# A relative-position attention, two causal stages and two mixtures: the second attention's scores in 64-row strips of high and low parts

## The chip, the cores and the metric

The kernel runs on one core of one Trainium2 chip. The metric is device time in microseconds (us); lower is better. Engines: TensorE (matmul, PE in the rows; PEld is its weight load), VectorE (DVE), ScalarE (ACT), GpSimd (POOL) and SyncE (SP, which issues most DMAs). They run on their own instruction streams and meet on semaphores.

## The reference

Input x is 4 batches of 512 tokens of 256 values. Four stages follow one another: an attention with relative positions against a context, a layer of causal attention and a mixture of 8 experts (2 per token), a cross attention with 16 heads of 64, and a mixture of 16 experts (6 per token). The change is in the causal attention of the second stage:

```python
def _causal_attention(nx, Wqkv, bqkv, Wo, bo):
    qkv = nx @ Wqkv + bqkv
    q, k, v = jnp.split(qkv, 3, axis=-1)           # each 16 heads of 16
    scores = jnp.einsum('bqhd,bkhd->bhqk', q, k) / jnp.sqrt(jnp.float32(HEAD_DIM))
    scores = jnp.where(causal, scores, jnp.finfo(scores.dtype).min)
    attn = jax.nn.softmax(scores, axis=-1)
    out = jnp.einsum('bhqk,bkhd->bqhd', attn, v).reshape(B, S, D)
    return out @ Wo + bo
```

nx is the layer norm of the first attention's result (with its residual). Inputs and outputs are float32.

## The kernel before

The second attention works in 16 units (NJ): four heads of one batch each, numbered n = 4 x batch + group. A unit has eight steps (NUF). Two sets of score products exist for each unit:

- the *natural rows*: queries on partitions, keys along the columns. Only their row maxima are used. VectorE takes them with one custom instruction per head and row block (`row_max`, L2101) into a tile MX. They run 12 steps (AHEAD) before the other set.
- the *transposed scores* (key products): keys on partitions, queries along the columns. ScalarE takes exp of them from PSUM into PTf (`exp_f`, L1686), and `values_f` (L1046) multiplies PTf with the values; a column of ones gives the sums.

The maxima reach the transposed scores through the contraction. A head has 16 values but sits in a strip of 32 rows: rows 16 to 31 hold the other head of the pair as zeros, a constant -1 in KP, and the maxima in QP. `max_to_rows` (L1071) turns MX on TensorE, and VectorE adds it into QP (L2106).

In `scores_f` (L1026, L1031) a step issues four fp32 matmuls, two heads of the transposed scores and two of the natural rows, each in a strip of 32 rows, so that the four run side by side. F_ROWS orders the natural row blocks so that a step's natural rows are as wide as its transposed scores:

```python
F_ROWS = (1, 1, 0, 0, 3, 3, 2, 2)
keys_mm = mm(STB[(2 * s + x) % 3][:, 0:S - c * P], KP[o:o + HQ8, hg, ...], QP[n % 4][o:o + HQ8, c * P:S], ...)
rows_mm = mm(PD[g % 2][:, x, 0:w], QP[m % 4][o:o + HQ8, r * P:r * P + P], KP[o:o + HQ8, hg, b * S:b * S + w], ...)
```

Banks: two pairs (PD[0], PD[1]) hold natural rows, three (STB) transposed scores, and one (MB) everything else in the order of the list M_USES: projections, values, turned maxima (`mx`), turned outputs (`ot`). TensorE waits before a step's key products for the first exponential of the step before (`f_ex`), and before natural rows for the maxima that free their banks (`f_max`). Every engine's order is written out by hand; at steps P_STEP, OT_STEP, MX_STEP and those of H_STEP1, H_STEP7 and Q_STEP the loop issues values, turned outputs, turned maxima and projections of later units: queries (`queries_f`, for two units at a time), keys (`hk`), values (`hv`), normalised tokens (`h`). A projection for keys or queries (L806) is copied from the bank by ScalarE twice, with one of two head masks (L1608, L1615).

GpSimd applies the causal mask to the diagonal of PTf (L718, `f_ca`), and in units 2 to 9 it also computes the residual Hs of the second stage behind every second mask (L707, L710). Before the stage it adds the first attention's outputs to X (L695). SP loads the projection weights WFs, WFv while the first attention ends, and all expert weights once the last scores are done (`f_st`). The first keys and queries (`f_hw`, `f_hr`) are projected within the last steps of the first attention (n == NJ in its loop), each into one of its free banks.

## Time and profile before

| | |
|---|---|
| median of 3 runs | 1791.98 us (1789.44 to 1795.83) |
| span of the profiled execution | 1784.9 us |
| what a run has around the span, by the median | 7.1 us |
| TensorE busy | 1648.8 us (92%) |
| VectorE busy | 1082.9 us (61%) |
| ScalarE busy | 898.1 us (50%) |
| GpSimd busy | 352.6 us (20%) |
| second attention, first to last exponential start | 377.4 to 621.6 us |

The profiled execution is one run; no separate time is given for it, so its span is set beside the median. Matmuls are pipelined and their ends are modelled: a matmul's duration reaches until its result is out, and the distance between two starts says how fast they follow. An fp32 matmul shows as two records, one for each pass. Times in brackets in the order of time are the idle time of the engine before the row and what ended it.

### The profile page before, as it was taken

The numbers are of one execution on the slowest core, as the hardware profiler recorded it, in microseconds if no ns is written. First come the engines' busy times: TensorE is split into PE (matmuls) and PEld (weight loads), VectorE is DVE, ScalarE is ACT, GpSimd is POOL, SyncE is SP. The second block draws the span as 40 slices with busy tenths as digits, with TensorE's granted clock in tenths as the row PEclk, the third lists the DMA queues.
The fourth block names the chain that finished last, engine by engine and source line by source line (L and its number), as shares of the span: only waits on it lengthen the run. The fifth ranks groups of instructions, "written<-read, shape, count | busy, mean of one in ns | idle before, by whom it ended". The sixth has DMA issues, their size and how long they took to land.

```text
span 1784.9 us, 32858 instructions
## 1 busy us (share of the span) xinstructions
PE 1648.8 (92%) x11314; PEld 1120.0 (63%) x11315; DVE 1082.9 (61%) x2944; ACT 898.1 (50%) x2088; POOL 352.6 (20%) x405
## 2 busy tenths in 40 slices
PE   8998989978888788999999799999999999989998
PEld 6555555533333386999999344566666566567887
DVE  4777677655556365222221687877776766767776
ACT  2888888635555422433334466665765765630000
POOL 1111111103432121111110421344232322110000
PEclk9999999889999887999999899999999999999999
DMA  8787778300000092111112311100010000020001
GB/s 304 260 284 258 275 256 292 118 1 1 1 1 1 10 382 79 38 36 35 38 36 68 111 50 31 59 19 25 24 30 24 19 25 18 13 83 1 1 0 47
DMA packets 74449, 149.64 MB, mean 84 GB/s; under 512 B 7024, under 2 KB 49648, under 8 KB 69840
## 3 DMA queue, kind: packets, MB, share of 16 engines
q1 hardware_dynamic: 70912, 138.64, 22.8%
q0 software_dynamic: 3408, 9.31, 1.8%
q8 instruction: 77, 1.26, 0.3%
q14 instruction: 52, 0.43, 0.1%
HBM read 96.68 MB, written 51.25 MB: 83 GB/s over the span
## 4 chain that ended last, share of the span: by engine, by line
PE 78%; DVE 9%; ACT 7%; issue 4%; DMA 1%; POOL 0%; SPq 0%; DVEq 0%; ACTq 0%; POOLq 0%
PE PS L1394 9%; PE PS L1231 8%; PE PS L1216 8%; PE PS L806 7%; PE PS L1349 6%; PE PS L1265 5%; PE PS L1364 5%; PE PS L1339 5%; PE PS L1026 5%; PE PS L873 4%; PE PS L895 3%; PE PS L1320 3%; PE PS L1046 2%; PE PS L906 2%; ACT PTf L1686 1%
## 5 line engine op out<-in xcount | busy, mean ns | idle before, releaser
L1813 ACT ACTIVATE P<-PS,nm 128x512 f32<-128x512 f32 x256 | 174.6, 694 | 108.4 <-DVE nm L2395 92.5
L1349 PEld LDWEIGHTS PS<-idf,P 128*128 128x128 f32 x1024 | 118.1, 143 | 98.8 <-issue 64.7
L2101 DVE CUSTOM_DVE_ANT_0 dump<-PS,maskw 128x256 f32<-128x256 f32 (+3 forms) x256 | 114.8, 487 | 92.3 <-PE PS L1031 87.1
L1349 PE MATMUL PS<-idf,P 128*128 128x128 f32 x1024 | 155.8, 282 | 12.4 <-ACT PTb L1823 11.0
L2012 DVE CUSTOM_DVE_ANT_0 SN<-PS,SR 128x128 f32<-128x128 f32 (+3 forms) x256 | 115.2, 487 | 83.8 <-PE PS L877 83.7
L2395 DVE TENSOR_REDUCE nm<-PS 128x2 f32<-128x1024 f32 x128 | 150.4, 1215 | 23.8 <-PE PS L1339 23.7
L1231 PEld LDWEIGHTS PS<-xT,W1c 128*128 128x128 f32 x1248 | 145.3, 192 | 4.2 <-ACT xT L1739 2.3
L1231 PE MATMUL PS<-xT,W1c 128*128 128x128 f32 x1248 | 145.8, 275 | 1.8 <-ACT xT L1739 1.8
L1026 PE MATMUL PS<-QP,KP 32*128 32x128 f32 (+3 forms) x512 | 107.6, 493 | 36.7 <-ACT PTf L1686 33.5
L1216 PE MATMUL PS<-EW,hT 128*128 x624 | 141.2, 379 | 0.0
L1686 ACT ACTIVATE PTf<-PS 128x512 f32<-128x512 f32 (+3 forms) x256 | 97.9, 435 | 82.7 <-PE PS L1026 82.6
L1565 ACT ACTIVATE SN<-SN,nm 128x128 f32<-128x128 f32 (+3 forms) x256 | 128.7, 555 | 7.2 <-DVE nm L2012 6.9
L1739 ACT ACTIVATE xT<-PS,cols 128x128 f32<-128x128 f32 x78 | 31.5, 454 | 197.0 <-PE PS L1206 197.0
L2286 DVE TENSOR_TENSOR ysb<-PS,fc2b 128x256 f32<-128x256 f32 x39 | 16.5, 424 | 187.3 <-PE PS L1216 187.3
L2615 DVE SCALAR_TENSOR_TENSOR X<-PS,gat,X 128x256 f32<-128x256 f32 x224 | 97.0, 479 | 46.2 <-PE PS L1394 45.3
L1216 PEld LDWEIGHTS PS<-EW,hT 128*128 128x128 f32 x624 | 115.6, 190 | 14.7 <-issue 0.4
L1364 PE MATMUL PS<-PTb,V 128*64 128x512 f32 x512 | 124.0, 605 | 0.0
L2404 DVE TENSOR_SCALAR P<-P,rc 128x512 f32<-128x512 f32 x256 | 121.1, 515 | 4.2
L873 PE MATMUL PS<-ErP,QPa 32*128 32x128 f32 (+3 forms) x448 | 91.2, 479 | 23.1 <-ACT EN L1558 14.0
L877 PE MATMUL PS<-Ka,QPa 32*128 32x512 f32 (+3 forms) x512 | 106.0, 488 | 2.7 <-DVE nm L2012 2.5
L1031 PE MATMUL PS<-KP,QP 32*128 32x384 f32 (+3 forms) x512 | 104.8, 492 | 4.0 <-DVE MX L2101 2.0
L895 PEld LDWEIGHTS PS<-idf,SN 128*128 128x128 f32 x640 | 68.5, 142 | 59.3 <-ACT SN L1565 35.1
(344 smaller groups left out, 3338.9 us busy)
## 6 DMA issues: line engine op xcount, KB each, us to landing
SR<-rel SPq DMA_DIRECT2D x16, 1024.0 KB, 8.0
rel<-EN SPq DMA_DIRECT2D x15, 1024.0 KB, 4.8
SR<-rel SPq DMA_DIRECT2D x16, 768.0 KB, 6.3
rel<-EN SPq DMA_DIRECT2D x15, 768.0 KB, 4.2
SR<-rel SPq DMA_DIRECT2D x16, 512.0 KB, 4.3
EW<-in_fc1T SPq DMA_DIRECT2D x8, 1024.0 KB, 11.8
EW<-in_fc2T SPq DMA_DIRECT2D x8, 1024.0 KB, 12.9
rel<-EN SPq DMA_DIRECT2D x15, 512.0 KB, 3.4
```

Source lines behind the costliest of these rows:

```text
L806: last = mm(bank[0:m, 0:n], w(k), src(k), start=(k == 0), stop=(k == DK - 1))
L873: rel_mm = mm(PD[0][:, i, 0:w], QPa[e // 2 % 3][o:o + HQ8, r * P:r * P + P], ErP[e % 2][o:o + HQ8, S - w:S], start=True, stop=True)
L895: last = nc.tensor.transpose(TRA[i % 2][:, o:o + P], SN[(2 * t + j) % 6][:, c * P:c * P + P], idf[:])
L1026: keys_mm = mm(STB[(2 * s + x) % 3][:, 0:S - c * P], KP[o:o + HQ8, hg, b * S + c * P:b * S + c * P + P], QP[n % 4][o:o + HQ8, c * P:S], st ...
L1216: last = mm(PS[5][:, 0:D], hT[s][:, f, :], EW[:, bass.ds(e, 1), o:o + D].rearrange("p e d -> p (e d)"), start=(f == 0), stop=(f == FK - 1))
L1231: ins = mm(PS[1 + 2 * s + f // 4][:, f % 4 * P:f % 4 * P + P], W1c[s][:, o:o + P], xT[:, k, :], start=(k == 0), stop=(k == DK - 1), skip_g ...
L1349: last = nc.tensor.transpose(TR1[j][:, c * P:c * P + P], P1[s % 4][:, j, c * P:c * P + P], idf[:])
L1364: last = mm(OUT1[o:o + DH1, :], V1[chunk % NV1][:, m % VG, o:o + DH1], PT1[m % 2][:, j, c, :], start=(c == 0), stop=(c == RT - 1), skip_gr ...
L1394: last = mm(PS[tb % 8][:].rearrange("p (e n) -> p e n", e=2), x[:, k, t], w[i][:, :, k, :], start=(n + k == 0), stop=(n + k == len(parts) ...
L1565: af(sn, sn, ACT.Exp, bias=nm[:, (ku + i) % 16:(ku + i) % 16 + 1], scale=-1.0).then_inc(a_ex, 1)
L1813: last = af(P1[s % 4][:, j, :], PD[s % 2][:, j, :], ACT.Exp, bias=nm1[:, s % 4, j:j + 1], accum_out=sm1[:, s % 4, j:j + 1])
L2395: v.tensor_reduce(nm1[:, s % 4, :], PD[s % 2][:], AX.X, ALU.max, negate=True).then_inc(c_max, 1)
```

## The change

Every head's 16 values are split into a high part (rounded to fp32r) and a low part (the rest). A head then sits in a strip of 64 rows: key rows hold high, high, low and, from row 48 (DQ) on, four constant rows; query rows hold high, low, high (in the order of KD and QD), so that one fp32r matmul sums the three products. MS holds the turned maxima, also as high and low parts, in the rows from 48; a second fp32r matmul with the same keys adds them to the transposed scores. The natural rows are one such matmul. A step has two heads, and each pair of matmuls runs in the two strips.

What else follows from it:

- ScalarE writes the high part of a projection (`high_h`, one copy with the bias), VectorE the low part (`low_h`), and SP copies 16-row pieces from HK and HQs into the strips KD (ring of 4) and QD (ring of 3): six DMAs for a unit's keys and six for its queries. Before that, GpSimd fills KD with the constants and QD with zeros once, ahead of the stage.
- The maxima go to a small tile mxs. GpSimd places them as high and low parts in MX (`place_max`), TensorE turns MX, ScalarE copies it to MS (`max_rows`).
- Natural rows have three single banks (NB), transposed scores three (STB), everything else two (MBF), used in turn.
- All four projections for keys and queries of a batch are made at once: batch 0 within the last steps of the first attention, each later one in the units of the batch before it (H_STEP). The values of batch 0 are projected before the first natural rows.
- F_ROWS puts wide natural rows beside narrow transposed scores.
- Heads are grouped as 4 x j + g, which changes the layout in which `outputs_f` writes ON. The weights WO are loaded after the last maximum.

The core of the diff (the entry's and the semaphores' edits and repeated lines are cut):

```diff
-F_ROWS = (1, 1, 0, 0, 3, 3, 2, 2)
-Q_STEP, P_STEP, OT_STEP, MX_STEP = 0, 2, 4, 6
-H_STEP1 = {0: ("hv", 0, 0), 1: ("hk", 1, 1), 3: ("hv", 1, 1), 5: ("hk", 2, 1), 7: ("hv", 2, 1), 9: ("hk", 3, 1),
-           11: ("hv", 3, 1)}
-H_STEP7 = {0: ("hk", 1, 0), 1: ("h", 6), 2: ("hv", 1, 0), 3: ("h", 7), 4: ("hk", 2, 0), 6: ("hv", 2, 0), 8: ("hk", 3, 0),
-           10: ("hv", 3, 0)}
+F_ROWS = (2, 2, 3, 3, 0, 0, 1, 1)
+P_STEP, OT_STEP, MX_STEP = 2, 4, 6
+HS, DQ, DM = P // 2, 3 * DH0, 4
+NKD, NQD = 4, 3
+H_STEP = {(2, 5): ("h", 6), (2, 7): ("h", 7)}
+for _b in range(B - 1):
+    H_STEP |= {(4 * _b, 7): ("hk", _b + 1, 0), (4 * _b + 1, 1): ("hk", _b + 1, 1), (4 * _b + 1, 3): ("hq", _b + 1, 0),
+               (4 * _b + 1, 5): ("hq", _b + 1, 1), (4 * _b + 2, 1): ("hv", _b + 1, 0), (4 * _b + 2, 3): ("hv", _b + 1, 1)}
+M_USES = [("hv", 0, 0), ("hv", 0, 1), ("mx", 0)]
...
+            def strips(kind, m, rings, halves, parts):
+                b, g = divmod(m, HGS)
+                to = rings[m % len(rings)]
+                for x in range(2):
+                    rows = slice(DH0 * (HQ * x + g), DH0 * (HQ * x + g) + DH0)
+                    for i, part in enumerate(parts):
+                        o = HS * x + DH0 * i
+                        sp.dma_start(to[o:o + DH0].bitcast(F32), halves[rows, part].bitcast(F32))\
+                            .then_inc(f_ld[kind][m % len(rings)], 16)
+
+            def key_strips(m):
+                if m < HGS:
+                    sp.wait_ge(f_hr, 2)
+                elif m % HGS == 0:
+                    m_done(sp, ("hk", m // HGS, 1))
+                if m < NKD:
+                    sp.wait_ge(f_kc, (2, 5, 8, 11)[m])
+                else:
+                    sp.wait_ge(f_st, (m - NKD + 1) * NUF)
+                strips("k", m, KD, HK, (0, 0, 1))
+
+            def query_strips(m):
+                if m < HGS:
+                    sp.wait_ge(f_hr, 4)
+                elif m % HGS == 0:
+                    m_done(sp, ("hq", m // HGS, 1))
+                if m < NQD:
+                    sp.wait_ge(f_kc, 3 * m + 3)
+                else:
+                    sp.wait_ge(f_st, (m - NQD + 1) * NUF)
+                strips("q", m, QD, HQs, (0, 1, 0))
+
+            key_strips(0)
+            for m in range(NJ):
+                query_strips(m)
+                if m + 1 < NJ:
+                    key_strips(m + 1)
...
+            def constant_rows(i):
+                for t in range(2):
+                    nc.gpsimd.tensor_scalar(KD[i][:, t], maskw[:], 0.0, kc[:, t:t + 1], ALU.mult, ALU.add).then_inc(f_kc, 1)
+
+            def zero_rows(i):
+                nc.gpsimd.memset(QD[i][:].bitcast(F32), 0.0).then_inc(f_kc, 1)
+
+            def place_max(n):
+                pool.wait_ge(f_max, n * NSU + NSU)
+                if n:
+                    pool.wait_ge(m_wrote(("mx", n - 1)), M_W["mx", n - 1])
+                at = lambda t, e: t.rearrange("p r (x c) -> p r x c", x=2)[:, :, :, DQ + e:DQ + DM + e:2]
+                nc.gpsimd.tensor_scalar(at(MX[:].bitcast(F32R), 0), mxs[n % 2][:], 1.0, None, ALU.mult).then_inc(f_kc, 1)
+                pool.wait_ge(f_kc, 2 * NKD + NQD + n + 1)
+                nc.gpsimd.tensor_tensor(at(MX[:], 1), mxs[n % 2][:], at(MX[:], 0), ALU.subtract).then_inc(f_mx, 1)
+
+            pool.wait_ge(s_bp, 3)
+            pool.wait_ge(a_tt, NJ * NSU)
+            constant_rows(0)
+            zero_rows(0)
+            constant_rows(1)
+            zero_rows(1)
+            pool.wait_ge(f_mz, 1)
+            pool.wait_ge(a_mr, len(A_USES))
+            pool.wait_ge(a_x, NJ)
+            constant_rows(2)
+            zero_rows(2)
+            constant_rows(3)
+            place_max(0)
...
+                    if n == NJ and u < 4:
+                        eight_heads_h(PS[u], "hk" if u < 2 else "hq", 0, u % 2).then_inc(f_hw, 1)
...
+                    bank = lambda x: STB[(2 * s + x) % 3][:, 0:S - c * P]
+                    keys = lambda x: KD[n % NKD][HS * x:HS * x + HS, t, c * P:c * P + P]
+                    for x in range(2):
+                        mm(bank(x), keys(x), QD[n % NQD][HS * x:HS * x + HS, t, c * P:S], start=True, stop=False)
+                    for x in range(2):
+                        last = mm(bank(x), keys(x), MS[n % 2][HS * x:HS * x + HS, c * P:S], start=False, stop=True)
+                    last.then_inc(f_st, 1)
                 if m < NJ:
-                    if i == 0 and m // 2:
-                        pe.wait_ge(f_mr, M_AT["q", m // 2] + 1)
-                    if i == 0 and m % 2 == 0 and m:
-                        pe.wait_ge(f_mr, M_AT["hk", m // HGS, m % HGS // 2] + 1)
-                    if g >= 2:
-                        pe.wait_ge(f_max, 2 * g - 2)
-                for x in range(2):
-                    if s >= 0:
-                        b, hg = divmod(n, HGS)
-                        o = HQ8 * (2 * pr + x)
-                        keys_mm = mm(STB[(2 * s + x) % 3][:, 0:S - c * P], KP[o:o + HQ8, hg, b * S + c * P:b * S + c * P + P],
-                                     QP[n % 4][o:o + HQ8, c * P:S], start=True, stop=True)
-                    if m < NJ:
-                        b, hg = divmod(m, HGS)
-                        o, r = HQ8 * (2 * (1 - pr) + x), F_ROWS[i]
-                        rows_mm = mm(PD[g % 2][:, x, 0:w], QP[m % 4][o:o + HQ8, r * P:r * P + P],
-                                     KP[o:o + HQ8, hg, b * S:b * S + w], start=True, stop=True)
-                if s >= 0:
-                    keys_mm.then_inc(f_st, 1)
-                if m < NJ:
-                    rows_mm.then_inc(f_nat, 1)
+                    if i == 0:
+                        pe.wait_ge(f_ld["k"][m % NKD], 96 * (m // NKD + 1))
+                        pe.wait_ge(f_ld["q"][m % NQD], 96 * (m // NQD + 1))
+                    if g >= 1:
+                        pe.wait_ge(f_max, 2 * g - 1)
+                    for x in range(2):
+                        last = mm(NB[(2 * g + x) % 3][:, 0:w], QD[m % NQD][HS * x:HS * x + HS, y, r * P:r * P + P],
+                                  KD[m % NKD][HS * x:HS * x + HS, y, 0:w], start=True, stop=True)
+                    last.then_inc(f_nat, 1)
...
+            def high_h(bank, kind, half):
+                to, c = (HK, COLS["bqkv"] + 2 + half) if kind == "hk" else (HQs, COLS["bqkv"] + half)
+                af(to[:, 0, half], bank[:], ACT.Identity, bias=cols[:, c:c + 1]).then_inc(f_hi, 1)
...
+            def max_rows(n):
+                bank = m_written(act, ("mx", n))
+                if n >= 2:
+                    act.wait_ge(f_st, (n - 1) * NUF)
+                af(MS[n % 2][:], bank[:], ACT.Copy).then_inc(m_read(("mx", n)), 1)
...
+            def low_h(bank, kind, half):
+                to, c = (HK, COLS["bqkv"] + 2 + half) if kind == "hk" else (HQs, COLS["bqkv"] + half)
+                return v.scalar_tensor_tensor(to[:, 1, half], bank[:], cols[:, c:c + 1], to[:, 0, half].bitcast(F32), ALU.add,
+                                              ALU.subtract)
```

## Rows read from the trace of the kernel before

**Rows 1.** The page, part 4: shares of the chain by line

```profile
PE PS L1394 9%; PE PS L1231 8%; PE PS L1216 8%; PE PS L806 7%; PE PS L1349 6%; PE PS L1265 5%; PE PS L1364 5%; PE PS L1339 5%; PE PS L1026 5%; PE PS L873 4%; PE PS L895 3%; PE PS L1320 3%; PE PS L1046 2%; PE PS L906 2%; ACT PTf L1686 1%
```

**Rows 2.** Order of time, TensorE, 512-column step: start, duration, operation, idle before

```profile
493.01 0.69 PE L1026 MATMUL PS<-QP,KP 32*128 32x512 f32 x1 [0.70 <-ACT PTf L1686]
493.54 0.59 PE L1026 MATMUL PS<-QP,KP 32*128 32x512 f32 x1
```

**Rows 3.** Order of time, ScalarE: exponentials of steps of 384 and 512 columns

```profile
484.40 0.87 ACT L1686 ACTIVATE PTf<-PS 128x384 f32<-128x384 f32 x2 [0.24 <-PE PS L1026]
492.36 1.08 ACT L1686 ACTIVATE PTf<-PS 128x512 f32<-128x512 f32 x2 [2.97 <-PE PS L1026]
494.20 1.09 ACT L1686 ACTIVATE PTf<-PS 128x512 f32<-128x512 f32 x2 [0.76 <-PE PS L1026]
```

**Rows 4.** Order of time, VectorE: the two maxima of a 512-column step

```profile
479.42 0.69 DVE L2101 CUSTOM_DVE_ANT_0 dump<-PS,maskw 128x512 f32<-128x512 f32 x1 [1.68 <-PE PS L1031]
480.04 0.08 DVE L2101 DVE_READ_ACCUMULATOR2_ANT MX<- 128x1 f32 x1
```

**Rows 5.** The page, part 5: all maxima; count, busy us, mean ns, idle before

```profile
L2101 DVE CUSTOM_DVE_ANT_0 dump<-PS,maskw 128x256 f32<-128x256 f32 (+3 forms) x256 | 114.8, 487 | 92.3 <-PE PS L1031 87.1
```

**Rows 6.** Order of time, ScalarE: the copies of a unit's sums, one a unit

```profile
499.28 0.60 ACT L1693 ACTIVATE OS<-PS 128x512 f32<-128x512 f32 x1 [1.42 <-PE PS L1046]
544.22 0.60 ACT L1693 ACTIVATE OS<-PS 128x512 f32<-128x512 f32 x1 [1.42 <-PE PS L1046]
559.94 0.60 ACT L1693 ACTIVATE OS<-PS 128x512 f32<-128x512 f32 x1 [1.42 <-PE PS L1046]
586.77 0.60 ACT L1693 ACTIVATE OS<-PS 128x512 f32<-128x512 f32 x1 [1.42 <-PE PS L1046]
599.48 0.60 ACT L1693 ACTIVATE OS<-PS 128x512 f32<-128x512 f32 x1 [1.42 <-PE PS L1046]
```

**Rows 7.** The chain in order of time: the values of one unit

```profile
496.93 2.28 PE PS L1046 x32
```

**Rows 8.** Order of time, TensorE, third attention: fp32r products in two 64-row strips

```profile
1302.98 0.50 PE L1339 MATMUL PS<-KH,QH 64*128 64x512 f32 x2
1303.32 0.39 PE L1339 MATMUL PS<-KH,QL 64*128 64x512 f32 x2
1303.55 0.40 PE L1339 MATMUL PS<-KL,QH 64*128 64x512 f32 x2
```

**Rows 9.** Order of time, entry into the second attention

```profile
350.68 3.60 PE L806 MATMUL PS<-NT,WFs 128*128 128x512 f32 x8
358.79 0.73 POOL L695 TENSOR_TENSOR X<-X,tmpA 128x256 f32<-128x256 f32 x1 [8.71 <-DVE tmpA L2039]
377.39 1.08 ACT L1686 ACTIVATE PTf<-PS 128x512 f32<-128x512 f32 x2 [9.24 <-PE PS L1026]
```

**Rows 10.** Groups by line, GpSimd: count, busy us, mean ns, idle before

```profile
L718 POOL TENSOR_SCALAR_AFFINE_SELECT PTf<-PTf 128x512 f32<-128x512 f32 x64 | 40.6, 635 | 190.5 <-ACT PTf L1686 190.5
L707 POOL TENSOR_SCALAR Hs<-X,mv,rsh 128x256 f32<-128x256 f32 x16 | 19.5, 1221 | 0.0
L710 POOL TENSOR_TENSOR Hs<-Hs,rows 128x256 f32<-128x256 f32 x16 | 11.6, 727 | 1.3
```

**Rows 11.** Order of time, SP: eight issues of 16 rows each

```profile
2.78 3.70 SPq L525 DMA_DIRECT2D ErP<-in_ErT  x8
```

**Rows 12.** DMA issues: count, KB each, us to landing

```profile
ErP<-in_ErT SPq DMA_DIRECT2D x8, 32.0 KB, 2.2
SR<-rel SPq DMA_DIRECT2D x16, 1024.0 KB, 8.0
```

**Rows 13.** Stretches: busy us of PE, PEld, DVE, ACT, POOL; clock; DMA share, GB/s

```profile
390.00:395.00 5.00, 2.87 (x29) 1.54 (x22) 4.01 (x23) 4.20 (x9) 0.63 (x1) 0.88 0.01 2
480.00:500.00 20.00, 17.59 (x168) 8.53 (x168) 11.54 (x45) 8.91 (x22) 7.00 (x9) 1.00 0.01 2
610.00:615.00 5.00, 4.41 (x20) 1.17 (x24) 0.00 (x0) 1.90 (x4) 0.63 (x1) 0.50 0.00 0
```

303 lines of the change are left out of this document (148 added, 155 removed).

## The prediction, made before the changed kernel was run

> **What bounds the kernel now.** I read the shares of the chain of waits first [rows 1]. They show TensorE lines throughout and none above 9%; the change touches only the second attention, so the question is what ends a wait there. Its score products (L1026), values (L1046) and part of the projections (L806) hold TensorE, and one exponential line (L1686) stands beside them. The order of time shows why. A 512-column step starts its products at 493.01, after 0.70 us in which TensorE waited for an exponential; each of its two fp32 passes is 0.53 us from the next [rows 2]. ScalarE starts the step's exponentials 1.19 us after TensorE started, and the exponentials of two such steps start 1.84 us apart [rows 3]. So the step is a ring: products 1.19 us until ScalarE sees them, first exponential 0.54 us (half of 1.09), 0.11 us back to TensorE. No engine is full. The copies of a unit's sums, one a unit (a group of four heads of one batch), give the pace: 12.71 us where nothing but the attention runs (586.77 to 599.48), 60.66 us for four units that also make one batch's projections (499.28 to 559.94), so 9.8 us a batch for those [rows 6].
>
> The ring explains the 12.71. Per 128 columns less, the two passes lose 0.21 us (a quarter of 2 x 0.427) and the exponential 0.105 (1.09/2 against 0.87/2 [rows 3]). Rings of 512, 384, 256 and 128 columns come to 1.84, 1.52, 1.20 and 0.87 us; two of each are 10.9. The values take 2.28 us [rows 7], of which 0.67 only fills the wait of its step: 1.6. Two groups of transposes add 0.1 to 0.2. Sum 12.6 against 12.71.
>
> **The change part by part.** *Scores.* Before, four matmuls of two passes run side by side in 32-row strips. After, a step has a pair of key products, a second pair that adds the row maxima, and a pair of natural rows, each pair in two 64-row strips, fp32r. The third attention has that shape: pairs of 512 columns start 0.23 us apart, the first after a change of layout 0.34 [rows 8]; the last one's duration, 0.39, is until its result is out. From start to ScalarE: 0.34 + 0.39 + 0.05 = 0.78 us instead of 1.19. Each 128 columns less take 0.053 us off a pair (0.23 for 512 is 0.213 for the columns and 0.02 beside them). With exponential and return the rings become 1.43, 1.22, 1.01 and 0.79 us.
>
> VectorE now becomes the second bound. Two maxima of 512 columns take 1.23 us (the first started at 479.42 and was out at 480.04 [rows 4], twice that); the mean of the four widths is 0.487 us [rows 5], so each 128 columns less take about 0.13 us off one. Three banks instead of four hold natural rows, so TensorE runs at most one and a half steps ahead. The new order puts 384 and 512 rows beside 256 and 128 keys: there VectorE wants 0.98 and 1.23 us and the ring 1.01 and 0.79. Some of it is caught up while TensorE waits for the next 512-column exponentials. I take 1.05 and 0.95 us. The sum is 2 x (1.43 + 1.22 + 1.05 + 0.95) = 9.3, values 1.6, transposes 0.15: 11.05 us a unit, 1.65 less. If nothing is caught up it is 11.6 (1.1 less); if VectorE never holds TensorE, 10.7 (2.0 less). Over 16 units: **-26.4** (-17.6 to -32).
>
> *Projections.* Before a batch costs 9.8 us for two queries, two keys and two value projections. The value pair costs 3.0 of it (544.22 to 559.94 is 15.72, less 12.71 [rows 6]) and stays. After there are four others, each 1.8 us of TensorE (3.60 for two [rows 9]) of which 0.6 fills a wait, plus 0.2 for the low part that VectorE makes behind ScalarE's high part, before its next maximum: 1.4 each, 5.6 a batch instead of 6.8. **-3.6** over three batches. ScalarE's two masked copies per projection become one, hidden as they were. Batch 0's second queries (1.4) and both its values (3.0) leave unit 0 for the entry, where TensorE waits anyway: **-4.4**.
>
> *Row maxima.* GpSimd now places them (two small operations) before TensorE can turn them. It takes its turn behind the causal mask and, in units 2 to 9, behind the residual of one token block: 0.64, 1.22 and 0.73 us [rows 10], and about 0.5 for its own two. That is 3.2 us after the exponentials of step 3; TensorE wants them about 2.2 us after. So TensorE, with all later products queued behind it, waits 1.0 us in eight units; a part lies under VectorE's 512-wide maxima: **+6** (0 to +9). In the other units GpSimd needs 1.3 us and hides. The copy of the turned maxima (ScalarE, 0.6) replaces VectorE's addition (0.69) and lies under the two widest maxima.
>
> *Entry.* Here the change loses. Four projections instead of two stand before the last values of the first attention: TensorE is full there, +3.6 us (3.60 for two [rows 9]). GpSimd's last addition ends at 359.5, so at 363.1 after. Only then does it fill the constant rows: two operations of 512 columns for each of four key buffers and a clear for each of three query buffers, and the strips are copied behind those. For one such operation no row exists: between 0.64 us (mask, 512 columns [rows 10]) and 2.4 (twice the 256-column tensor-scalar with two operands). SP needs 0.46 us an issue (3.70 for eight [rows 11]), six for keys and six for queries: 5.5 us, and 2.2 to land [rows 12]. Natural rows then start at 372 to 376, eight steps of maxima take 6.7 us, and placing, turning and copying the maxima some 3. The first exponential comes at 382.3 to 388.6 instead of 377.39. **+8** (+5 to +11). The first keys and values projected there lie in TensorE's wait.
>
> *Strips in the steady part.* SP copies a unit's query strips when the unit three before is done with its keys: 6 x 0.46 + 2.2 = 5.0 us. TensorE wants them at step 4 of the next unit, after 2 x 1.43 + 2 x 1.22 + 1.6 = 6.9 us. Hidden, with 1.9 us to spare; the key strips have a unit more. The later load of the output weights and the other layout of the outputs cost nothing: nobody needs the one before the stage ends, and the other has as many elements. Everything behind the stage shifts with it, since the expert weights are loaded when the last scores are done.
>
> Sum: -26.4 - 3.6 - 4.4 + 6 + 8 = **-20.4 us**. The profiled execution's span is 1784.9; the median of the runs is 1791.98, 7.1 more, which I leave standing around it. 1792.0 - 20.4 = **1771.6**, a span of about 1764.5. With all bounds at their good ends 1754, at their bad ends 1789.
>
> **Rivals.** (A) *Weight loads lie open.* In 32-row strips a pass of 512 columns is 0.53 us where its columns take 0.427 [rows 2]: 0.105 us are open. If that also came with the second pair and the rows pair of each step (0.105 to 0.21 x 8 x 16 = 13 to 27 us), the time is 1785 to 1798, middle 1791. Against it: 512-wide pairs in the same two strips stand 0.23 apart [rows 8]; for narrow ones no row exists. Chance 0.09. The Trainium skill (TensorE: Matmul & The Clock Gate, section The mechanism) has a rule that speaks for this rival: a weight load runs beside matmuls in flight only when its row group differs, and here successive pairs use the same two groups. By that rule every pair would pay; the 512-column rows above don't bear it out.
>
> (B) *Slower: the clock falls.* TensorE does fewer columns in about the same number of waits. In the steady part the granted clock is 1.00 (2.4 GHz) at 88% busy; it was 0.88 in a stretch at 57% busy, and 0.50 (1.2 GHz) when the natural rows had ended, though records then filled 88% of the time [rows 13]. At 0.50 a new unit's rings are 2.1, 1.8, 1.5 and 1.3 us, the values 3.8 and the projections twice as long: some 23 us against 13.1. It decides from 2 units on (20 us gained); four units make it 1812. Against it: columns per time, which I work out as about 70% of a unit against 73% before. Chance 0.09.
>
> (C) *Slower: the query strips come late.* It decides when issue and landing pass 6.9 us. With the 8.0 us landing of a large read [rows 12] each of 13 units waits 3.9: 1822. Against it: these are 64 KB, and the queue is empty. Chance 0.05.
>
> **How the numbers follow.** The forecast has 0.77. I call within 0.3% (5.4 us) no change. The forecast is faster in 0.74, the same in 0.03 (its bad end, above 1786.6). A: 0.05 the same, 0.04 slower. B: slower. C: 0.02 the same, 0.03 slower. Faster 0.74, same 0.10, slower 0.16. The range reaches from the forecast's good end into A: 1753 to 1798.
>
> **What would show it.** Copies of sums about 11 us apart in the last units and 52 in a batch instead of 60.7; ScalarE's 512-column steps 1.4 us apart; pairs 0.23 us apart in L1026's successor; first exponential 5 to 11 us later; a wait of the turning transposes for GpSimd only in units 2 to 9; no wait for strips after unit 2. Steps with 512 rows at 1.23 us would put me at 1780. Any steady stretch at a clock below 1.00 proves B, open loads at narrow widths A, TensorE waiting on strips C. If the whole gain is above 35 us, VectorE never held the ring.

## The result, and the profile after

Forecast 1771.6 us, measured **1795.56 us** (median of 11 runs) against 1790.91 (median of 11) for the kernel before: ratio 1.0025 [1.0017, 1.0033]. The forecast's sign was wrong: 20.4 us less was expected, 4.65 more came. That lies within the 0.3% that I had called no change, with an interval that just excludes a ratio of 1. One of the 11 runs of the changed kernel ran in a slower state (2348.94 us); the ratio leaves it out.

The profiled executions' spans are 1784.9 us before and 1796.8 after, 11.9 apart. Some 5 of that is chance: in a second profile of the kernel before, the unchanged first attention ended 5.6 us later (below).

The page of the kernel after, part 4, shares of the chain by line:

```profile
PE PS L1479 9%; PE PS L1316 8%; PE PS L1301 8%; PE PS L912 6%; PE PS L1434 6%; PE PS L1350 5%; PE PS L1449 5%; PE PS L1424 5%; PE PS L979 4%; PE PS L1001 3%; PE PS L1405 3%; PE PS L1140 3%; PE PS L1012 2%; PE PS L1116 2%; ACT PTf L1769 1%
```

It answers to [rows 1]: the score line's 5% has become 2% (L1116, beside L1118 and L1127, too small for this list), the values' 2% has become 3% (L1140). Work did leave TensorE; the time did not follow. The copies of sums (order of time, ScalarE) show where:

```profile
559.75 0.60 ACT L1776 ACTIVATE OS<-PS 128x512 f32<-128x512 f32 x1 [1.55 <-PE PS L1140]
...
573.18 0.60 ACT L1776 ACTIVATE OS<-PS 128x512 f32<-128x512 f32 x1 [1.55 <-PE PS L1140]
...
587.63 0.60 ACT L1776 ACTIVATE OS<-PS 128x512 f32<-128x512 f32 x1 [2.88 <-PE PS L1140]
...
601.29 0.60 ACT L1776 ACTIVATE OS<-PS 128x512 f32<-128x512 f32 x1 [2.87 <-PE PS L1140]
...
614.93 0.60 ACT L1776 ACTIVATE OS<-PS 128x512 f32<-128x512 f32 x1 [2.88 <-PE PS L1140]
```

Against [rows 6]: a unit without projections takes 13.64 us (601.29 to 614.93), not 12.71 as before and not 11.05 as forecast. From the first copy to the fourteenth the 13 intervals add up to 195.81 us, against 192.86 before. Stretches of the same kernel (columns as in [rows 13]):

```profile
559.75:573.18 13.43, 11.34 (x98) 6.85 (x100) 8.38 (x35) 7.14 (x18) 3.01 (x6) 1.00 0.30 49
573.18:587.63 14.45, 11.89 (x90) 6.38 (x92) 7.73 (x34) 7.14 (x19) 2.99 (x6) 0.76 0.43 72
...
605.29:607.29 2.00, 1.79 (x12) 1.07 (x12) 1.88 (x9) 0.97 (x4) 0.16 (x1) 1.00 0.00 0
607.29:609.29 2.00, 1.36 (x10) 0.95 (x12) 1.64 (x8) 1.21 (x3) 0.63 (x1) 1.00 0.00 0
609.29:611.29 2.00, 1.37 (x14) 0.77 (x10) 0.51 (x4) 1.20 (x3) 0.55 (x1) 0.78 0.00 0
611.29:613.29 2.00, 2.00 (x14) 0.48 (x16) 0.78 (x4) 0.76 (x2) 0.09 (x1) 0.50 0.03 8
```

The granted clock falls from 1.00 to 0.50 (2.4 to 1.2 GHz) in all five of the 13 intervals that hold no projection (the copies from the third to the fourth, the seventh to the eighth, and the last three intervals); a sixth had 0.98. Before, it was 1.00 in all 13, in both profiles. Here the fall comes behind a stretch in which TensorE was 68% busy, but that share alone doesn't tell it: the kernel before kept 1.00 through 2 us at 65% (594.77 to 596.77). The fall hits the values, the longest work of a unit:

```profile
570.77 2.35 PE L1140 MATMUL PS<-PTf,VE 128*17 128x512 f32 x32
...
583.99 3.57 PE L1140 MATMUL PS<-PTf,VE 128*17 128x512 f32 x32
```

Which intervals fall is in part chance. The same steady stage was profiled twice more, in e3 and e7 (below): the last three intervals fell in all three profiles, each of the two earlier ones in two of three, and the 13 intervals add up to 196.7 and 192.8 us there. Put together from the intervals that one of the three profiles shows at 1.00, with 12.02 us for the last three (worked out below), a full clock would give about 182.5 us.

ScalarE's exponentials in one unit, steps 3 to 7 and then 0 to 2 of the next, at full clock up to 609.6:

```profile
601.81 0.87 ACT L1769 ACTIVATE PTf<-PS 128x384 f32<-128x384 f32 x2
602.90 0.66 ACT L1769 ACTIVATE PTf<-PS 128x256 f32<-128x256 f32 x2 [0.22 <-PE PS L1118]
604.09 0.66 ACT L1769 ACTIVATE PTf<-PS 128x256 f32<-128x256 f32 x2 [0.53 <-PE PS L1118]
605.00 0.45 ACT L1769 ACTIVATE PTf<-PS 128x128 f32<-128x128 f32 x2 [0.26 <-PE PS L1118]
...
606.98 0.44 ACT L1769 ACTIVATE PTf<-PS 128x128 f32<-128x128 f32 x2
608.16 1.08 ACT L1769 ACTIVATE PTf<-PS 128x512 f32<-128x512 f32 x2 [0.75 <-PE PS L1118]
609.59 1.09 ACT L1769 ACTIVATE PTf<-PS 128x512 f32<-128x512 f32 x2 [0.34 <-PE PS L1118]
611.17 0.87 ACT L1769 ACTIVATE PTf<-PS 128x384 f32<-128x384 f32 x2 [0.50 <-PE PS L1118]
```

Their starts are 1.09, 1.19, 0.91, **1.98**, 1.18 and 1.43 us apart, then 1.58 where the clock has begun to fall (1.31 at full clock in e4). The forecast had 1.22, 1.05, 1.05, **0.95**, 0.95, 1.43 and 1.43. The rings were about right; one place, steps 6 to 7, took twice its share. The chain of waits through it, in order of time (start, us, what):

```profile
603.16 0.56 DVE dump L2190
...
603.73 0.47 DVE dump L2190
...
604.21 0.18 DVE rec L2198
...
604.75 0.55 DVE dump L2190
...
605.36 0.50 PE PS L1127 x2
605.86 0.60 PE PS L1161 x4
...
606.48 0.40 ACT MS L1760
...
606.98 0.28 ACT PTf L1769
```

VectorE is late with the 384-column maxima of two steps and the unit's output division; TensorE holds back the next natural rows (L1127), and behind them stand the four transposes of the maxima and the keys of step 7.

In four of the 13 intervals (the third, fourth, seventh and eighth, in units that also have the residual on GpSimd, units 3, 4, 7 and 8) the same place takes 2.24 us, and the transposes wait for GpSimd:

```profile
455.85 0.63 PE L1161 MATMUL PS<-idf,MX 128*128 128x128 f32 x4 [0.22 <-POOL MX L801]
```

Where such a unit has no projection, it takes 12.30 us at full clock (12.29 in e7, 12.31 in e3), not 12.02.

The entry, from the last addition to X to the first exponential (order of time; GpSimd, SP, TensorE, ScalarE):

```profile
367.51 0.73 POOL L770 TENSOR_TENSOR X<-X,tmpA 128x256 f32<-128x256 f32 x1 [12.47 <-DVE tmpA L2122]
368.23 1.37 POOL L789 TENSOR_SCALAR KD<-maskw,kc 128x512 fp32r<-128x512 f32 x2
...
369.67 3.78 SPq L623 DMA_DIRECT2D KD<-HK  x6
373.56 3.69 SPq L623 DMA_DIRECT2D QD<-HQs  x6
...
379.20 0.69 PE L1127 MATMUL PS<-KD,QD 64*128 64x384 f32 x2 [6.13 <-DMA QD<-HQs]
...
389.14 0.69 PE L1127 MATMUL PS<-KD,QD 64*128 64x384 f32 x2 [0.62 <-DVE mxs L2190]
...
395.44 1.08 ACT L1769 ACTIVATE PTf<-PS 128x512 f32<-128x512 f32 x2 [2.52 <-PE PS L1118]
```

27.9 us, against 18.6 before [rows 9]. The clock is 0.50 from 380 to 410 (0.83 in the 5 us before, in which TensorE begins to work again at 379.2).

### The profile page after: what moved, and what is told of

Its sections match the earlier page's. It is cut to its first block, busy times and chain, and to the rows that moved or that the text cites. A ratio compares the mean times of both kernels' runs of the same rounds, so it can differ in the third digit from the quotient of the medians.

```text
span 1796.8 us, 32572 instructions
## 1 busy us (share of the span) xinstructions
PE 1660.4 (92%) x11058; PEld 1149.5 (64%) x11059; DVE 1083.9 (60%) x2945; ACT 892.6 (50%) x2088; POOL 368.2 (20%) x448
## 3 DMA queue, kind: packets, MB, share of 16 engines
q1 hardware_dynamic: 77056, 151.24, 27.1%
q8 instruction: 75, 1.23, 0.3%
## 4 chain that ended last, share of the span: by engine, by line
PE 76%; DVE 9%; ACT 7%; issue 5%; POOL 1%; DMA 1%; SPq 0%; DVEq 0%; ACTq 0%; POOLq 0%
PE PS L1479 9%; PE PS L1316 8%; PE PS L1301 8%; PE PS L912 6%; PE PS L1434 6%; PE PS L1350 5%; PE PS L1449 5%; PE PS L1424 5%; PE PS L979 4%; PE PS L1001 3%; PE PS L1405 3%; PE PS L1140 3%; PE PS L1012 2%; PE PS L1116 2%; ACT PTf L1769 1%
## 5 line engine op out<-in xcount | busy, mean ns | idle before, releaser
L2477 DVE TENSOR_REDUCE nm<-PS 128x2 f32<-128x1024 f32 x128 | 150.6, 1216 | 23.7 <-PE PS L1424 23.6
L2190 DVE CUSTOM_DVE_ANT_0 dump<-PS,maskw 128x384 f32<-128x384 f32 (+3 forms) x256 | 114.5, 488 | 76.1 <-PE PS L1127 70.7
L979 PE MATMUL PS<-ErP,QPa 32*128 32x128 f32 (+3 forms) x448 | 92.3, 483 | 23.1 <-ACT EN L1643 12.8
L1001 PE MATMUL PS<-idf,SN 128*128 128x128 f32 x640 | 100.6, 289 | 1.5 <-DVE PTa L2111 1.4
L1904 ACT ACTIVATE PTb<-PS 128x512 f32<-128x512 f32 x128 | 76.9, 600 | 34.2 <-PE PS L1434 34.1
## 6 DMA issues: line engine op xcount, KB each, us to landing
EW<-in_fc2T SPq DMA_DIRECT2D x8, 1024.0 KB, 12.3
```

The costliest lines, as they stand in the source:

```text
L979: rel_mm = mm(PD[0][:, i, 0:w], QPa[e // 2 % 3][o:o + HQ8, r * P:r * P + P], ErP[e % 2][o:o + HQ8, S - w:S], start=True, stop=True)
L1001: last = nc.tensor.transpose(TRA[i % 2][:, o:o + P], SN[(2 * t + j) % 6][:, c * P:c * P + P], idf[:])
L2477: v.tensor_reduce(nm1[:, s % 4, :], PD[s % 2][:], AX.X, ALU.max, negate=True).then_inc(c_max, 1)
```

## Experiments

Each kernel is the changed one with the edit shown, unless another is named. Theory V: VectorE's maxima set the pace. Theory C: the fallen clock does. "Unit" is an interval between copies of sums where no projection runs; a "late" one is one of the last three of the 13 intervals; "steady sum" is the sum of the first 13 intervals (195.81 us in the changed kernel, 192.86 in the one before). e9, e10, e11 and e14 have 4 runs each, e13 and e15 5, e5 one, the others 10.

**e1, order of the widths.** Natural rows of 512 stand beside turned 512 columns.

```diff
-F_ROWS = (2, 2, 3, 3, 0, 0, 1, 1)
+F_ROWS = (1, 1, 0, 0, 3, 3, 2, 2)
```

> The changed kernel with one line as before: natural rows again as wide as the step's transposed scores, F_ROWS = (1, 1, 0, 0, 3, 3, 2, 2). Theory V (VectorE's pace): in the changed kernel a unit without projections takes about 12.0 us at full clock, not the 11.05 forecast, because steps 4 to 7 pile up four wide pairs of maxima and the outputs' division on VectorE; with equal widths VectorE's 1.23 us fits under the 1.42 us ring of a 512-column step, so such a unit falls to about 11 us where the clock is 1.00, and the median by up to 13 us if the clock is low for no longer than it was. Theory C (the clock): the steps with narrow products stand together again with even less for TensorE to do, so the granted clock falls for as long or longer (18 us of the changed kernel's stage I put down to it); the median is then within 6 us of the changed kernel's 1795.6, 1788 to 1801.

Measured 1797.53 us, ratio to before 1.0039 [1.002, 1.0058]. A unit at full clock takes 11.56 to 11.58 us, 0.44 less than 12.02 (the sum of the steps above at full clock, with 2.94 for the step with the values). But six of 13 intervals fell to a clock of 0.67 to 0.90, among them 15.77 and 15.51 us, and the steady sum is 195.0. So the change's order of widths costs time at full clock, and what e1 gains on it is lost to the clock. The median is in the range of theory C.

**e2, unread products.** A pair of 512-column products that nobody reads, ahead of the keys in steps 4 to 7 and of the natural rows in steps 0 to 3.

```diff
+                    if c >= 2:
+                        for x in range(2):
+                            mm(STB[(2 * s + x) % 3][:, 0:S], keys(x), QD[n % NQD][HS * x:HS * x + HS, t, 0:S], start=True, stop=True)
...
+                    if s >= 0 and c < 2:
+                        for x in range(2):
+                            mm(NB[(2 * g + x) % 3][:, 0:S], ...)
```

> The changed kernel with fill: before the real products, TensorE computes a pair of 512 columns into the same two free banks, which the real ones overwrite; before the transposed scores in steps 4 to 7 and before the natural rows in steps 0 to 3. 256 pairs, each 0.23 us, none of them read. Theory C (the clock): the granted clock stays at 1.00 through the steady part; units that took 13.6 to 15.9 us without projections take 12.0 to 12.6, and the median falls by 8 to 18 us against the changed kernel, to 1778 to 1788. Theory V (VectorE's pace alone): the fill only adds; up to 0.23 us on each of the steps where TensorE is not waiting, the median at 1796 to 1812.

Measured 1793.93, 1.0004 [0.9988, 1.0021]. All 13 intervals at 1.00; steady sum 191.5. TensorE does more work and the stage takes less time: the clock was a cost. The last three units are 12.64, so the filling itself costs 0.6 each, and the median is only 1.6 us below the changed kernel's, not the 8 to 18 of theory C.

**e3, unread products in the entry.** Seven products of 512 columns, fp32, after the projections of the entry.

```diff
+            for _ in range(7):
+                mm(PS[3][:, 0:S], idf[:], NT[:, 0, 0:S], start=True, stop=True)
```

> The changed kernel with seven 512-column fp32 products into an unused bank in TensorE's wait for the first strips (6.1 us idle, after which the clock was 0.50 for some 35 us). None is read. Theory C: the wait no longer drops the clock at once; natural rows of unit 0 run in about 8 us instead of 9.9, the first unit's values and projections at full clock; the first copy of sums comes 3 to 6 us earlier, the median 2 to 6 us lower (1789 to 1794). If the natural rows alone are too thin to hold the clock, it falls right after and the gain is 0 to 2 us. A theory by which the entry is only the issue of strips and GpSimd's fills expects no change.

Measured 1798.93, 1.0032 [1.0012, 1.0051]: higher than the changed kernel, where theory C expected 2 to 6 us less. The fill held the clock at 1.00 up to about 382.5 us; then, among the natural rows, it fell to 0.50 all the same (0.69 on average between 375 and 395). The first three distances between natural rows at full clock are 1.10, 1.10 and 1.30 us instead of 1.34, 1.35 and 1.59. From the last addition (368.16) to the first exponential (395.29) it is 27.1 us for 27.9. So full clock in three steps was worth 0.8 us; the run doesn't show what it would give in all of them.

**e4, short maxima.** VectorE reads only the 128 diagonal columns of each block (the maxima over the other columns are left out).

```diff
-                    v.tensor_tensor_reduce(dump[k % 2][:, 0:w], NB[k % 3][:, 0:w], maskw[:, S - w:S], ...
+                    v.tensor_tensor_reduce(dump[k % 2][:, 0:P], NB[k % 3][:, w - P:w], maskw[:, S - P:S], ...
```

> The changed kernel, whose maxima read only the diagonal 128 columns of each natural row block (the maxima, and so the output, are not the reference's): each of the 256 takes 0.29 us. It takes VectorE's share out and leaves everything else. Theory V: steps 4 to 7 are no longer held, units lose 1 us or more: the median 13 to 20 us lower, 1775 to 1783, unless the clock takes it back. Theory C alone: the clock is as low as before or lower, since TensorE's work per time is what counts; the median falls by less than 6 us (1790 to 1796). The entry's eight first steps also lose 3 to 4 us in either theory.

Measured 1785.48, 0.996 [0.9947, 0.9974]. Units 11.38 to 11.42 at full clock. ScalarE's exponentials of steps 5, 6, 7 and 0:

```profile
587.16 0.66 ACT L1769 ACTIVATE PTf<-PS 128x256 f32<-128x256 f32 x2 [0.53 <-PE PS L1118]
588.07 0.45 ACT L1769 ACTIVATE PTf<-PS 128x128 f32<-128x128 f32 x2 [0.26 <-PE PS L1118]
...
589.43 0.44 ACT L1769 ACTIVATE PTf<-PS 128x128 f32<-128x128 f32 x2
590.61 1.09 ACT L1769 ACTIVATE PTf<-PS 128x512 f32<-128x512 f32 x2 [0.74 <-PE PS L1118]
```

The 1.98 has become 1.36 and every other distance is the same to 0.02. So VectorE costs 0.62 us in such a unit, at that place alone. It is not so in every unit: in the four that wait for GpSimd, steps 6 to 7 still take 2.24 us and the unit 12.30, and the transposes now wait longer:

```profile
508.64 0.63 PE L1161 MATMUL PS<-idf,MX 128*128 128x128 f32 x4 [0.85 <-POOL MX L801]
```

At full clock the gain over the 13 intervals is about 5 us, not 13 times 0.62. The median is 10.1 us below the changed kernel's and lies above theory V's 1775 to 1783. 12 of 13 intervals stayed at 1.00, all three late ones and both earlier ones without projections among them. The interval with this wait of 0.85 us stayed at 1.00 too, so a single rest of that length did not bring the clock down here.

**e5, the kernel before again**, unchanged.

> The kernel before, unchanged, for a second profile. Its first profile showed the first attention's copies of OSa 21.4 to 22.0 us apart where the kernels with the strips showed up to 23.5, though that stage is the same in all. If the dips of the granted clock there are chance from one execution to the next, this profile shows some of them too and the last addition to X begins later than 358.8 us. If they belong to the change, it begins within 1 us of 358.8. In the second attention both theories expect the steady period of before: copies of sums about 15.7 and 14.1 us apart at a granted clock of 1.00.

The last addition to X, and the first exponential behind it:

```profile
364.41 0.73 POOL L695 TENSOR_TENSOR X<-X,tmpA 128x256 f32<-128x256 f32 x1 [8.72 <-DVE tmpA L2039]
...
384.60 1.09 ACT L1686 ACTIVATE PTf<-PS 128x512 f32<-128x512 f32 x2 [10.90 <-PE PS L1026]
```

5.6 us later than in [rows 9], by dips of the clock in the first attention: chance, as the one theory had it. From addition to exponential it is 20.2 us here and 18.6 there. The steady sum is 192.87 against 192.86. The steady part repeats; entry and end move by 1 to 3 us.

**e6, widths and unread products in every step.** e1's F_ROWS, and the pair ahead of the natural rows in all steps.

> The changed kernel with natural and turned row blocks of the same width beside each other (F_ROWS 1,1,0,0,3,3,2,2), and a pair of 512-column products that nobody reads ahead of the natural rows in every step; 16 more products a unit, about 1.4 us of TensorE a step. Theory V (the pace is VectorE's maxima, and TensorE has room): units without projections take 11.6 to 12.0 us, as same width alone gave at full clock. Theory C (a TensorE that rests lets the clock fall): with the fills the clock stays at 1.00 in every unit, the sum of the 13 steady units falls from about 208 us to about 190, and the median from 1797.5 to about 1782. If the fills themselves are on the path (TensorE has no room), units take 12.7 or more and the median stays above 1790.

Measured 1793.25, 1.0012 [0.9982, 1.0043]: the expectation's last case. Clock 1.00 in all 13, but units of 12.8 and a steady sum of 193.7. As much filling as this is on the path. (The 208 us of the expectation counts one interval more; over 13, e1 had 195.0.)

**e7, early constants.** GpSimd writes the constant rows of the first two key buffers and clears the first query buffer ahead of its last addition to X.

```diff
+                if n == NJ + 1:
+                    pool.wait_ge(s_bp, 3)
+                    pool.wait_ge(a_tt, NJ * NSU)
+                    constant_rows(0)
+                    zero_rows(0)
+                    constant_rows(1)
...
-            pool.wait_ge(s_bp, 3)
-            pool.wait_ge(a_tt, NJ * NSU)
-            constant_rows(0)
-            zero_rows(0)
-            constant_rows(1)
+            pool.wait_ge(a_x, NJ)
             zero_rows(1)
```

> The changed kernel with the entry's fills moved: GpSimd writes the constant rows of the first two KD buffers and clears the first QD ahead of its last addition to X, the second QD behind it. Theory E (the entry's chain is fills, then six strip DMAs at 0.62 us each on SP's queue, then 1.95 us of landing, then the natural rows): the strips go out at about 362 us instead of 369.7, the natural rows begin when the last addition and the strips are both done, at 370 to 373 instead of 379.2, and the median falls by 5 to 10 us, to about 1788. Rival: the entry waits for something else (the projections of unit 0, the low clock), and the first exp stays within 2 us of 395.4 and the median at 1795.

Measured 1787.71, 0.9974 [0.9944, 1.0004]; against the changed kernel's median 7.9 us less. SP, TensorE and ScalarE:

```profile
358.71 3.77 SPq L623 DMA_DIRECT2D KD<-HK  x6
...
370.93 0.44 PE L1129 MATMUL PS<-KD,QD 64*128 64x384 f32 x2
...
386.26 1.09 ACT L1771 ACTIVATE PTf<-PS 128x512 f32<-128x512 f32 x2 [2.52 <-PE PS L1120]
```

The natural rows follow the projections without a gap, where TensorE had waited 6.13 us for strips. From the last addition (365.45) to the first exponential it is 20.8 us instead of 27.9.

**e8, e6 and e7 together.**

> Both of the former edits at once: same widths with the unread pairs in every step, and the constants and the clearing ahead of the last addition. If the clock's loss and the entry's chain are two separate costs, the gains add: 12 to 15 us from the one and 5 to 10 from the other, a median of about 1774, below both the kernel before and the changed one. If the entry gives nothing, about 1782; if neither does, 1795.

Measured 1788.20, 0.9982 [0.9953, 1.0011]: 5.0 less than e6, and far above the 1774 expected if the gains add. The entry's gain adds; fills of this size had none to give.

**e9, e10, e11, light fills.** e7 with an unread pair in steps 4 to 7 alone: 256 columns and e1's widths (e9), 256 columns and the changed kernel's widths (e10), 512 columns and e1's widths (e11).

```diff
+                    if c >= 2:
+                        for x in range(2):
+                            mm(STB[(2 * s + x) % 3][:, 0:256], keys(x), QD[n % NQD][HS * x:HS * x + HS, t, 0:256], start=True, stop=True)
```

> The changed kernel with early constants, same widths, and a pair of 256-column products that nobody reads ahead of the keys in steps 4 to 7 alone, half the columns of the former fills. If the clock's loss needs only a little work of TensorE to be kept away: granted clock 1.00 in all units, units without projections 11.6 to 12.0 us, the 13 steady units together about 182 us, median about 1780. If light fills are too little: 0.50 stretches come back, units of 13.6 to 15.8, median 1788 or more.

> The same as the last, with the changed kernel's own order of widths (2,2,3,3,0,0,1,1). Against the last it prices the order of the widths at a clock that is (if the fills hold it) the same in both. By theory V the order costs 0.4 to 0.6 us a unit either way and this one is the slower, by 5 to 8 us; if what counted was only that one order lets TensorE rest longer, both are within 2 us.

> As e9, but with 512 columns a product in the fills of steps 4 to 7. It shows from which size fills are on the path: by the rings of 512 columns at full clock TensorE has 0.2 to 0.5 us a step left in steps 4 to 7, so this one should take 12.2 to 12.7 us a unit at a clock of 1.00, and a median of about 1786.

Measured, against a before of 1791.28: e9 **1774.02**, 0.9915 [0.9896, 0.9933]; e10 1777.31, 0.9923 [0.9906, 0.9939]; e11 1775.10, 0.992 [0.9902, 0.9939]. Units at full clock 11.62, 12.15 and 12.06 us. Steady sums 183.1 and 185.3 for e9 and e10, each with one interval at a fallen clock (0.77, 0.88), and 184.4 for e11, whose 13 intervals all stay at 1.00. The order of widths is worth 0.53 us in a late unit at full clock but only 2.2 in the steady sum: the four intervals in which the transposes wait for GpSimd gain nothing (12.39 for 12.33) or lose 0.4 us (15.62 for 15.20), and e9's one fall cost more (14.60 for 13.94). The medians of four runs don't tell the three apart, and e11 came out better than its expectation of 12.2 to 12.7 us a unit and 1786. All three beat both kernels.

**e12, the kernel before with short maxima** (the edit of e4 on the kernel before; the same maxima are left out).

> The kernel before, with the row maxima of the second attention taken over the 128 diagonal columns only (the others are left out), as e4 did it to the changed kernel, where it saved about 0.65 us a unit at the same clock and 10 us in all. Theory V (VectorE's maxima set the pace only once the scores are cheaper): here TensorE sets the unit, which stays at 12.7 us without projections and the median within 3 us of the kernel before. If VectorE already set the pace before the change, it falls by 5 us or more.

Measured 1789.87, 0.9996 [0.9985, 1.0007]; units 12.71 as ever. VectorE's maxima were no bound before: the change made them one.

**e13, light fills alone.** The changed kernel with the diff of e10 and nothing else.

> The changed kernel with one edit: a pair of 256-column products that nobody reads ahead of the keys in steps 4 to 7. Theory C: the granted clock stays at 1.00 in nearly all units between the copies of sums, the 13 intervals add up to about 184 us instead of 195.8, and the median falls by 10 to 12 us, to about 1784 to 1786. If the gain of the last runs came from the early constants and the widths, it stays above 1790.

Measured 1785.04, 0.9959 [0.9944, 0.9975], 10.5 us below the changed kernel. The steady sum is 185.3, also 10.5 less. A stretch from copy to copy, same columns as above:

```profile
567.54:579.70 12.16, 9.93 (x98) 5.82 (x100) 7.70 (x34) 7.14 (x19) 3.00 (x6) 1.00 0.35 59
```

**e14, e15, late copy.** e9 and e10 with ScalarE's copy of the turned maxima behind the exponentials of step 7.

```diff
-                    if u == MX_STEP and n + 1 < NJ:
+                    if u == MX_STEP + 1 and n + 1 < NJ:
                         max_rows(n + 1)
```

> e9 (early constants, same widths, light fills) with ScalarE's copy of the turned maxima behind the exponentials of step 7 instead of ahead of them. There VectorE has only 128-column maxima beside step 7, so what stood between the exponentials of steps 6 and 7 (1.19 us for 0.87 of a 128-column ring) should be the copy: if so, steps 6 to 7 take 0.8 to 0.9 us, 7 to the next 0 takes 1.2 to 1.5, and a unit 11.3 to 11.6 us. If the next unit's first row pair waits for the copy, the unit stays at 11.6 or grows.

> e10 (early constants, light fills, the changed kernel's order of widths) with the same move of the copy. If the copy costs the 0.5 us that it lasts, steps 6 to 7 take 1.25 us instead of 1.75 and the unit 11.7 instead of 12.15. If VectorE's four 512-column maxima set that place, as theory V has it, steps 6 and 7 together still take about 2.9 us to the next step 0 (1.75 and 1.19 now), and the unit stays within 0.1 us of 12.15.

Measured 1783.25, 0.9951 [0.9934, 0.9967], and 1799.01, 1.0046 [1.0032, 1.006]: 9 and 22 us slower than without the move. In e14 steps 6 to 7 keep their 1.18 us, the next step 0 comes 1.76 us later instead of 1.19, a late unit takes 12.17 us at full clock, and three intervals fell to 0.77 to 0.88 where e9 had one. ScalarE in e15, steps 6, 7 and 0, and TensorE's wait ahead of step 0:

```profile
587.41 0.45 ACT L1774 ACTIVATE PTf<-PS 128x128 f32<-128x128 f32 x2 [0.37 <-PE PS L1123]
589.15 0.45 ACT L1774 ACTIVATE PTf<-PS 128x128 f32<-128x128 f32 x2 [1.29 <-PE PS L1123]
590.91 1.09 ACT L1774 ACTIVATE PTf<-PS 128x512 f32<-128x512 f32 x2 [0.83 <-PE PS L1123]
...
590.14 0.50 PE L1121 MATMUL PS<-QD,KD 64*128 64x512 f32 x2 [0.75 <-ACT MS L1765]
```

Steps 6 to 7 keep their 1.74, so the copy doesn't set that place. What is left beside VectorE is TensorE's own order: rows pair, four transposes (0.6 us), keys; no run tests that by itself. Both theories in the expectation for e15 missed: the next step 0 comes 0.57 us later (1.76 for 1.19), since TensorE now waits for the copy. A unit at full clock is 12.75, and five of 13 intervals fell to 0.91 or less, where e10 had one. The steady sum grew by 16.0. The added wait is about 5 us of it: 0.46 to 0.59 us in nine intervals, none in the four in which step 0 already came later than 1.7 us in e10. The rest, about 11 us, came with the fallen clock.

## Why the prediction was wrong

"Expected" and "had" are the prediction's; +/- is against it. From the changed kernel's trace, with what the runs above isolate:

| term | expected | measured | off by |
|---|---|---|---|
| scores, 16 units | -26.4 | -11.0 (16 x (12.71 - 12.02)) | +15.4 |
| clock in the steady part | 0 (rival B, 0.09) | +13.3 | +13.3 |
| placing the maxima | +6 | +1.1 (4 x (12.30 - 12.02)) | -4.9 |
| projections, three batches | -3.6 | -2.5 | +1.1 |
| entry | +8 | +12.3 | +4.3 |
| unit 0 beside the scores | -4.4 | -3.7 | +0.7 |
| last two units beside the scores | 0 | -4.3 | -4.3 |

They add up to 25.6; the medians miss by 25.0 (4.65 + 20.4). The first four rows go by the full-clock sum of 182.5 us. In the last three rows before is the mean of its two profiles, which differ there by 1.6 to 2.7 us; I can't divide them further. Projections: the two batches that lie wholly within the 13 intervals cost 8.6 us each at full clock (the first of them: 57.25 us for four units, less four times 12.02 and two waits of 0.27) for 9.8 before, which is the 1.2 of the forecast; the three intervals before them, with the end of the first batch, gained only 0.1. Entry: 3.8 for the projections and 8.5 (27.9 less the mean of 18.6 and 20.2). Unit 0: from the first exponential to the first copy of sums 23.7 us for 28.1, less 0.7 of scores. Last two: 19.95 for 25.7, less 1.4 of scores.

**Scores: the mechanism was right, the second bound was sized too small.** The two passes side by side became pairs 0.23 to 0.34 us apart, as the third attention had shown [rows 8]. TensorE in the changed kernel, a step of 512 columns with its narrow natural rows:

```profile
608.81 0.50 PE L1116 MATMUL PS<-QD,KD 64*128 64x512 f32 x2 [0.54 <-ACT PTf L1769]
609.15 0.40 PE L1118 MATMUL PS<-MS,KD 64*128 64x512 f32 x2
609.38 0.22 PE L1127 MATMUL PS<-KD,QD 64*128 64x128 f32 x2
```

0.34 and 0.23, and the 512 ring is 1.43, as forecast; the other distances but one (1.31, 1.09, 1.19, 0.91 and 1.18 us) add up to 5.7, forecast 5.7. The step that failed is "Some of it is caught up ... I take 1.05 and 0.95". VectorE's debt from steps 4 to 6, with the output division (0.25 and 0.43 us) that the sum left out, falls due at one place: steps 6 to 7 take 1.98, where 0.95 was forecast. e4 puts 0.62 of the missing 0.97 a unit (12.02 for 11.05) on VectorE, e12 shows that this bound was not there before, and e1 that another order of widths gives back 0.44. Of the rest, the 1.36 of e4 is still 0.41 above 0.95: there the four transposes (0.6 us of TensorE's queue) stand ahead of the keys; they were priced at 0.1 to 0.2 for two groups. That this is the 0.41 is argued from the order of the rows, not tested. "Steps with 512 rows at 1.23 us would put me at 1780" named the danger, but with half its size.

**Rival B was real and had a chance of 0.09.** Its sign was right: any steady stretch below 1.00 proves it, I wrote, and all five intervals without projections fell. In this profile it costs 13.3 us: 3.6 in each of two, 2.4, 1.6 and 1.6, and 0.4 in the intervals behind the first two; in the profiles of e7 and e3 it cost some 10 and 14. e13 took most of it away, alone, and gained 10.5, with fills that cost 0.13 us a unit (12.15 for 12.02) and one interval that still fell by 1.6. My price was for whole units at 1.2 GHz (10 us a unit); in fact, by the mean clock of the intervals, a fall lasted 3 to 10 us, over the values each time. Against it I had set that columns per time were about the same, 70% for 73%. That average over a unit can't tell them apart: TensorE is busy 77% of a unit before (9.81 of 12.71 us, and the clock stays) and 79% in e4 (9.06 of 11.40, and stays); an interval of e4 at 74% (9.12 of 12.30 us, with the wait of 0.85 us in it) stayed as well, and so did one of the changed kernel's stage at 76% (9.37 of 12.29, in e7). Nor is it the rests alone: a late unit of the changed kernel rests TensorE six times, 2.6 us in all and 0.64 at most, the kernel before five times, 2.9 us in all and 0.70 at most. Shown is the direction among variants of the changed kernel: unread products held the clock (in all 13 intervals in e2, e6, e8 and e11, in 12 in e9, e10 and e13), e4, with one rest of 0.40 us less in a late unit, kept it in 12, and e14 and e15, with 0.57 us more, lost it more often. What decides between 1.00 and 0.50 is open, and in part it is chance from one execution to the next.

**Entry.** The projections cost what was forecast (11.30 us between two copies of the first attention's results became 15.06, +3.8 for +3.6). The natural rows began 11.0 us after the last addition's end, between the 8.9 and 12.9 of the forecast, though SP needed 0.62 us an issue, not 0.46 as in [rows 11] (those copies come from DRAM, these from SBUF; no run shows whether that is why), 7.5 us for 12 of them. What was too small is what follows: eight steps of rows and maxima took 9.9 us instead of 6.7, since with three banks TensorE and VectorE take turns (0.69 and 0.66 us for 384 columns at 1.2 GHz; e3 shows 0.24 to 0.29 us a step less at full clock), and from there to the first exponential 6.3 instead of 3. e7 removed the wait for the strips and gained 7.1 us of it. The forecast's own terms also don't give its range: natural rows at 372 to 376 with 6.7 and 3 us behind them end at 381.7 to 385.7, 4.3 to 8.3 us later than before, not at 382.3 to 388.6; and the bounds of all terms add up to 1757 and 1786, not 1754 and 1789.

**Placing the maxima.** All waits of the turning transposes for GpSimd (line, engine waited for, us, times, longest) are

```profile
PE PS L1161 <- POOL MX L801: 0.9, 4, 0.2
```

0.9 us, not 6, and in four units, not eight. The mechanism was as forecast: behind the mask (0.64) and the residual (1.22 and 0.73) GpSimd is done 3.3 us after the exponentials of step 3 (505.37 to 508.64 in e7), forecast 3.2. What the forecast called "a part lies under VectorE's 512-wide maxima" was nearly all of it: at this place VectorE is almost as late, and GpSimd adds 0.27 us (2.24 for 1.98). e4 lays it open: with short maxima the wait is about 0.85 us each time, 3.4 in all. So this bound stands right behind VectorE's. The term, too large by 4.9 us, hid a fifth of the miss.

**Rivals A and C** did not occur: a pair of 256 columns in the same two strips follows another after 0.12 us (603.76 to 603.88) with no open weight load; and no unit of the steady part waited for strips. The Trainium skill's rule that a weight load overlaps matmuls in flight only when its row group differs (TensorE: Matmul & The Clock Gate, The mechanism) is not borne out by these rows or by [rows 8].

## What to carry to other kernels

When an engine's work in a loop shrinks, list every other engine's work step by step, small operations (a division, a transpose group) included, and add it up over the narrowest place of the unit, not over the unit: the debt is paid at one step. Look at the engine behind that one too: here GpSimd's placing took over in four units as soon as VectorE was relieved. Then look at the granted clock: a stage that sat at full clock with waits between its products can lose it when the products get cheaper, and a few unread products (256 columns, where the waits are) cost 0.13 us a unit and gave back 10. And an entry is worked off in order: the constant rows that nobody waits for can be written before the last thing that everybody waits for (7 to 8 us here). With the old order of widths, light fills and early constants the changed kernel takes 1774 us (e9) against 1791. That is near the 1771.6 of the forecast, but by edits that the forecast did not have.

## What the runs showed of the hardware

- Kernels that did more work on TensorE ran faster: e13 issues 8 more products a unit and is 10.5 us shorter, with one interval of 13 at a fallen clock (0.88) where the changed kernel had six (0.68 to 0.98).
- SP took 0.62 us for each issue of a strip copy within SBUF (3.69 to 3.78 for six), against 0.46 for loads of 16 rows from DRAM [rows 11].
- A tensor-scalar of GpSimd over 512 columns with one operand per partition took 0.68 us (1.37 for two), near the mask's 0.64 [rows 10] and far from the forecast's upper bound of 2.4.
- The granted clock also dips in the first attention, in other places from one execution to the next: its copies stood 21.96 us apart in one profile and 23.55 in another of the same kernel. One profile's span is no measure of a change of 5 us.
- The clock fell with no rest of TensorE above 0.64 us in the unit (changed kernel, 601.29 to 614.93), and stayed at 1.00 with one of 0.85 us in it (e4, 503.83 to 516.13).
